# Adaptive conditioning and a mixture of experts: rows of h turned by VectorE instead of TensorE, logits turned by transposes

## The chip, the cores and the metric

The kernel runs on one core of a Trainium2 chip. The metric is the time of one execution on the device in microseconds (us), taken as the median of several runs. Engines are named as in the profile: PE is TensorE (PEld its weight loads), DVE is VectorE, ACT is ScalarE, POOL is GpSimd, SP is SyncE, which here only issues DMAs.

## The reference, cut to what matters

There are 8192 tokens (128 batches of 64) of 512 features. First a conditioning layer gives h, then an expert layer works on h, and x is added.

```python
q_emb = relu(q @ W3 + b3)
h = relu(((n * v + v_sum) * q_emb[:, None, :]) @ W2 + b2)      # v is x, v_sum over the 64 tokens of a batch
scores = softmax(h @ gate_w.T); topk_w, topk_i = top_k(scores, 6)   # 64 experts
# each expert takes its first 64 tokens in order; the others are dropped
y = sum over the kept (token, expert): topk_w * (silu(h @ w_gate[e]) * (h @ w_up[e])) @ w_down[e]
shared = silu(h @ sw_gate) * (h @ sw_up) @ sw_down             # 704 wide
out = x + y + shared
```

## The kernel before

The tokens are worked through in 16 chunks of 512. Matrix products in full precision are made of three products of parts: each operand is split in a high part (`hh`, `xmh`, `w2h`) and the rest (`hl`, `xml`, `w2l`), and `three` (L1107 to L1109) adds high x high, high x low, low x high.

The first stage goes through the chunks in pairs a, b (`body`). For each chunk PE turns x (`transpose_x`, L1117), DVE makes the modulated input (`take_xt`, with L781, L788, L796, L800), ACT and DVE split it, and PE forms h transposed, features on the partitions, in four tiles of 128 features (`cond_tile`). ACT takes each tile out of PSUM with bias and relu into `h32` (L594) and copies it to `hh` (L578); DVE makes `hl = h32 - hh` (`split_h`, by the helper line L760). The gate's logits come from `logits_raw` (L1151 to L1155), whose 128 output rows are the high and low part of the gate's weights times hh, with hl times the high part added to the first 64; ACT copies them to `lsb`, and `logits` (L1165) turns them and adds the two halves at once by a product with `fold`, two identities on top of each other. `route` on DVE finds the best six experts, z is the logits less their maximum, ACT exponentiates it, `score` normalises. `merge` keeps the first 64 tokens of each expert. PE then runs the shared expert's gate and up tiles (`gu_tile`, 11 a chunk) and down tiles (`down_tile`, four) for the odd chunks; for the even ones h is stored to `hT` and their shared expert is done in the second stage.

The second stage also needs h with tokens on the rows, as rows of a `table` in DRAM from which POOL gathers the tokens of two experts at a time. That is what `rows_tile` is for: for each of the four feature tiles of a chunk PE makes four transposes of 128x128 out of `h32` into bank 7, ACT copies them to `hrow` (`take_rows`), and after four tiles SP stores 1 MB (`store_rows`).

Each engine's program is an order written out by hand, with semaphores between them. An engine works strictly in its order. For the odd chunk b of a pair PE has: cond_tile 0, logits of a, cond_tile 1, rows_tile 0, cond_tile 2, rows_tile 1, cond_tile 3, rows_tile 2, one down_tile, a transpose of x, rows_tile 3, another transpose, logits_raw, gate and up tiles. DVE has: route of a, two split_h, score of a, split_h 2, merge 5, split_h 3, merge 6, take_down, merge 7, take_xt of the next chunk, route of b. For an even chunk c PE has cond_tile 0 and 1, rows_tile 0, two transposes of x, cond_tile 2, rows_tile 1, cond_tile 3, rows_tile 2, down_tile 0, rows_tile 3, logits_raw; DVE has score, split_h 0 and 1, take_xt, split_h 2 and 3.

In the first 70 us weights are loaded in seven pieces and split: ACT copies the high part, POOL subtracts (L528). The first piece is W2 (`w2h`, `w2l`), the last two `sdh` and `sdl`. take_cond on ACT is held until the zero rows are stored (`pads_stored`).

Of the kernel before, what the change touches and what calls it, by code (L numbers as in the profile page):

```python
# [7 lines left out]
ALU = mybir.AluOpType  # L8
# [6 lines left out]
CAP = 64  # L15
EXP_UNDERFLOW = -87.3365447
# [4 lines left out]
def adaln_moe_ffn_kernel(nc, x, cond, W3, b3, W2, b2, gate_w, w_gate, w_up, w_down,  # L21
# [42 lines left out]
    with ctx:  # L64
# [50 lines left out]
        hrow = keep("hrow", [P, J, D])  # L115
# [15 lines left out]
        fold = keep("fold", [P, E])  # L131
# [47 lines left out]
        zrows = hrow[0:CAP, :, :].rearrange("p j d -> p (j d)")  # L179
# [3 lines left out]
        class Sems:  # L183
# [16 lines left out]
            fold_ready = sem("fold_ready")  # L200
# [11 lines left out]
            rows_filled = sem("rows_filled")  # L212
# [53 lines left out]
        sgv = sw_gate.rearrange("(kc p) i -> p kc i", p=P)  # L266
        suv = sw_up.rearrange("(kc p) i -> p kc i", p=P)
# [6 lines left out]
        pieces = [([(w2v, stage_view(0, KC, D))], [(w2h[:, :, :], w2l[:, :, :], stage_view(0, KC, D))])]  # L274
# [70 lines left out]
        def _(sp):  # L345
# [14 lines left out]
            def load_hT(u):  # L360
                sp.wait_ge(s.hT_stored, 16 * (u + 1))
                if u == 0:
                    sp.wait_ge(s.rows_filled, KC * NCH)
# [50 lines left out]
            with nc.allow_non_contiguous_dma(reason="two vectors of 512 elements, once"):  # L414
                sp.dma_start(b3c[:, :], b3.rearrange("(k p) -> p k", p=P)).then_inc(s.bias_loaded, 16)
                sp.dma_start(b2c[:, :], b2.rearrange("(k p) -> p k", p=P)).then_inc(s.bias_loaded, 16)
# [61 lines left out]
            sp.wait_ge(s.rows_stored, 16 * NCH)  # L478
# [35 lines left out]
        def _(pool):  # L514
# [40 lines left out]
            pool.wait_ge(s.rows_stored, 16 * NCH)  # L555
# [20 lines left out]
        def _(act):  # L576
# [9 lines left out]
            def take_cond(n, oc):  # L586
                act.wait_ge(s.cond_filled, KC * n + oc + 1)
                wait(act, s.rows_filled, KC * (n - 1) + oc + 1)
# [62 lines left out]
            act.wait_ge(s.pads_stored, 32)  # L651
# [3 lines left out]
            take_rows(0, 0)  # L655
            take_cond(0, 2)
            take_rows(0, 1)
# [3 lines left out]
            take_rows(0, 2)  # L661
            take_lraw(0)
            take_rows(0, 3)
# [3 lines left out]
            def body(i):  # L667
# [5 lines left out]
                take_rows(b, 0)  # L673
                take_cond(b, 2)
                take_rows(b, 1)
# [3 lines left out]
                take_rows(b, 2)  # L679
                if i == 0:  # L680
                    split_piece(6)
                take_rows(b, 3)
# [23 lines left out]
                if more:  # L706
# [3 lines left out]
                    take_rows(c, 0)  # L710
                    take_cond(c, 2)
                    take_rows(c, 1)
# [3 lines left out]
                    take_rows(c, 2)  # L716
                    split_xm(d, 2)
                    take_rows(c, 3)
# [39 lines left out]
        def _(dve):  # L758
# [48 lines left out]

            def split_h(n, oc):
                dve.wait_ge(s.hh_ready, KC * n + oc + 1)
# [40 lines left out]
            def route(n):  # L850
                lg = logits_bank(n)[:, 0:J * E].rearrange("p (j e) -> p j e", j=J)
                dve.wait_ge(s.logits_filled, n + 1)
                for j in range(J):
# [5 lines left out]
                link(nc.vector.tensor_tensor(z[:, :, :], lg, top[:, :, 0:1].to_broadcast([P, J, E]), ALU.subtract))  # L859
# [166 lines left out]
            def slot_rows():  # L1026
# [11 lines left out]
            nc.vector.tensor_copy(fold[0:E, :], ident[0:E, 0:E]).then_inc(s.fold_ready, 1)  # L1038
            nc.vector.tensor_copy(fold[E:P, :], ident[E:P, E:P]).then_inc(s.fold_ready, 1)
# [10 lines left out]
                  gw2[:, :, 0:E]).then_inc(s.gw2_ready, 1)  # L1050
            split_h(0, 0)
# [53 lines left out]
        def _(pe):  # L1105
# [29 lines left out]
            def rows_tile(n, oc):  # L1135
                pe.wait_ge(s.cond_taken, KC * n + oc + 1)
                wait(pe, s.rows_taken, KC * n + oc)
                if oc == 0 and n >= 2:
                    pe.wait_ge(s.merge_step, MERGE_STEPS * (n // 2 - 1) + 1)
                for j in range(J):  # L1140
                    op = nc.tensor.transpose(bank[7][:, j * P:(j + 1) * P], h32[:, oc, j * P:(j + 1) * P], ident[:, :])  # L1141
                op.then_inc(s.rows_filled, 1)

            def logits_raw(n):
# [4 lines left out]
                for k in range(KC):  # L1149
                    if k == KC - 1:  # L1150
                        nc.tensor.matmul(o[0:E, :], gw2[:, k, 0:E], hl[:, k, :], start=False, stop=False)  # L1151
                        op = nc.tensor.matmul(o[:, :], gw2[:, k, :], hh[:, k, :], start=False, stop=True)
                    else:
                        nc.tensor.matmul(o[:, :], gw2[:, k, :], hh[:, k, :], start=(k == 0), stop=False)  # L1154
                        nc.tensor.matmul(o[0:E, :], gw2[:, k, 0:E], hl[:, k, :], start=False, stop=False)  # L1155
                op.then_inc(s.lraw_filled, 1)

            def logits(n):
# [28 lines left out]
            def ranksT(i):  # L1187
                pe.wait_ge(s.ranks_ready, 2 * i + 2)
                pe.wait_ge(s.rows_taken, KC * (2 * i + 2))
# [222 lines left out]
```

## Time and profile before

| what | value |
|---|---|
| median of 3 runs | 1317.76 us (1317.4 to 1317.92) |
| the profiled execution | 1318.17 us |
| its span in the profile | 1316.3 us |
| mean granted clock of PE | 0.993 |
| busy: PE, DVE, ACT, POOL | 1291.7, 663.3, 370.2, 169.2 us |
| HBM traffic over the span | 196 GB/s |

The profile is of one execution. Busy times are sums over the instructions of an engine; matmuls are pipelined, so a row's mean duration is longer than the pitch from one to the next, and the pitch is read from the chain of work or from starts in the timeline. PEclk is the granted clock of PE as a share of 2.4 GHz. First stage: to about 680 us; second stage: the rest.

### The profile page before, as it was taken

What the parts mean: (1) busy time and instruction counts of PE and PEld (TensorE: products, weight loads), DVE (VectorE), ACT (ScalarE), POOL (GpSimd) and SP (SyncE); (2) the same over time, 40 slices, a digit from 0 to 9 for tenths busy, and PEclk for the clock granted to TensorE, in tenths of its full rate; (3) what the DMA queues carried; (4) which work ended last, traced back from release to release, by engine and by line L of the source; (5) the groups of instructions that cost most, each with busy time, mean ns of one, the idle gap of its engine ahead of it and who ended that gap; (6) DMA issues with size and microseconds to landing.
All of it is one profiled execution on the core that took longest, in us unless ns stands there. A gap on an engine that the chain in (4) does not pass through costs nothing.

```text
span 1316.3 us, 16591 instructions
## 1 busy us (share of the span) xinstructions
PE 1291.7 (98%) x6424; PEld 962.8 (73%) x6424; DVE 663.3 (50%) x1430; ACT 370.2 (28%) x611; POOL 169.2 (13%) x129
## 2 busy tenths in 40 slices
PE   4899999999999999999999999999999999999999
PEld 3688888888888888888876666666666667666666
DVE  6685785857758577684742323223232232323322
ACT  2734443343433434334322112111121111211111
POOL 2400000000000000000001222222222222222220
PEclk7999999999999999999999999999999999999999
DMA  6434305142150522503666897997989889798952
GB/s 199 166 111 141 123 37 174 55 172 93 53 194 18 176 89 76 188 5 140 230 209 216 256 320 243 307 317 221 317 291 282 285 268 333 233 298 281 292 138 76
DMA packets 97006, 250.94 MB, mean 191 GB/s; under 512 B 17632, under 2 KB 17760, under 8 KB 94752
## 3 DMA queue, kind: packets, MB, share of 16 engines
q1 hardware_dynamic: 85440, 224.70, 47.9%
q0 software_dynamic: 11488, 25.17, 9.5%
q8 instruction: 52, 0.85, 0.3%
q14 instruction: 26, 0.21, 0.0%
HBM read 197.14 MB, written 61.10 MB: 196 GB/s over the span
## 4 chain that ended last, share of the span: by engine, by line
PE 97%; DVE 1%; ACT 1%; DMA 0%; issue 0%; SPq 0%; ACTq 0%; DVEq 0%
PE bank L1107 23%; PE bank L1109 22%; PE bank L1108 22%; PE bank L1331 12%; PE bank L1354 7%; PE bank L1141 2%; PE bank L1117 2%; PE bank L1313 1%; PE bank L1215 1%; PE bank L1214 1%; PE bank L1165 1%; PE bank L1154 1%; PE bank L1155 1%; PE bank L1340 1%; DVE xm L800 0%; DMA w3s<-in_L_cond_W_dram 0%
## 5 line engine op out<-in xcount | busy, mean ns | idle before, releaser
L1107 PE MATMUL bank<-hh,gu 128*128 128x512 f32 x704 | 281.3, 400 | 0.0
L1109 PE MATMUL bank<-hh,gu 128*128 128x512 f32 x704 | 274.6, 390 | 0.0
L1108 PE MATMUL bank<-hl,gu 128*128 128x512 f32 x704 | 274.3, 390 | 0.0
L1107 PEld LDWEIGHTS bank<-hh,gu 128*128 128x128 f32 x704 | 132.5, 188 | 38.0 <-issue 12.8
L817 DVE TENSOR_TENSOR prod<-bank,prod 128x512 f32<-128x512 f32 x96 | 66.3, 690 | 176.8 <-PE bank L1109 156.5
L1109 PEld LDWEIGHTS bank<-hh,gu 128*128 128x128 f32 x704 | 132.1, 188 | 28.6
L1108 PEld LDWEIGHTS bank<-hl,gu 128*128 128x128 f32 x704 | 132.4, 188 | 25.3
L578 ACT ACTIVATE ah<-prod 128x512 fp32r<-128x512 f32 x96 | 60.6, 632 | 262.0 <-DVE prod L817 262.0
L1107 PE MATMUL bank<-sdh,ah 128*128 128x512 f32 x320 | 128.2, 401 | 0.0
L1109 PE MATMUL bank<-sdh,al 128*128 128x512 f32 x320 | 124.9, 390 | 0.0
L1108 PE MATMUL bank<-sdl,ah 128*128 128x512 f32 x320 | 124.8, 390 | 0.0
L533 POOL DMA_INDIRECT hg<-table,idx_pair x32 | 33.1, 1033 | 704.5 <-DVE idx_hi L1029 606.4
L1107 PE MATMUL bank<-xmh,w2h 128*128 128x512 f32 x256 | 105.4, 412 | 1.8 <-DVE xml L760 1.3
L621 ACT ACTIVATE prod<-bank 128x512 f32<-128x512 f32 x96 | 57.3, 597 | 176.1 <-PE bank L1109 175.9
L1109 PE MATMUL bank<-xmh,w2l 128*128 128x512 f32 x256 | 101.3, 396 | 0.0
L1108 PE MATMUL bank<-xml,w2h 128*128 128x512 f32 x256 | 100.8, 394 | 0.0
L1354 PE MATMUL bank<-wd,eactT 128*64 128x512 f32 (+1 forms) x384 | 89.6, 601 | 0.0
L760 DVE TENSOR_TENSOR hl<-h,hh 128x512 fp32r<-128x512 f32 x96 | 66.8, 717 | 41.5 <-ACT hh L578 41.1
L594 ACT ACTIVATE h<-bank,b2c 128x512 f32<-128x512 f32 x64 | 44.0, 687 | 137.2 <-PE bank L1109 137.2
L1331 PE MATMUL bank<-wg,hgt 128*64 128x352 f32 x512 | 81.2, 459 | 0.0
L1331 PE MATMUL bank<-wu,hgt 128*64 128x352 f32 x512 | 81.2, 459 | 0.0
L1084 DVE TENSOR_SCALAR ysc<-bank,hg 64x512 f32<-64x512 f32 x64 | 48.0, 750 | 61.2 <-PE bank L1354 56.1
(123 smaller groups left out, 1705.8 us busy)
## 6 DMA issues: line engine op xcount, KB each, us to landing
wg<-in_L_ffn_w_gate_dram SPq DMA_DIRECT2D x64, 704.0 KB, 9.2
wu<-in_L_ffn_w_up_dram SPq DMA_DIRECT2D x64, 704.0 KB, 11.2
wd<-in_L_ffn_w_down_dram SPq DMA_DIRECT2D x64, 512.0 KB, 5.3
x<-in_x_dram SPq DMA_DIRECT2D x16, 1024.0 KB, 8.7
table<-hrow SPq DMA_DIRECT2D x16, 1024.0 KB, 4.4
wd<-in_L_ffn_w_down_dram SPq DMA_DIRECT2D x64, 192.0 KB, 6.1
out_dram<-outst SPq DMA_DIRECT2D x36, 256.0 KB, 3.4
hT<-h SPq DMA_DIRECT2D x8, 1024.0 KB, 3.9
```

Of the source, the lines that this page charges most:

```text
L533: nc.gpsimd.indirect_dma_start(out=hg[p % 3][:, :], out_offset=None, in_=table, in_offset=bass.IndirectOffsetOnAxis(ap=idx_pair[:, p:p + 1 ...
L578: return nc.scalar.activation(o, i, ACT.Copy)
L594: nc.scalar.activation(h32[:, oc, :], bank[5 + oc % 2][:, :], ACT.Relu, bias=b2c[:, oc:oc + 1]).then_inc(s.cond_taken, 1)
L621: nc.scalar.activation(prod[0:m, i % 2, :], bank[t % 3][0:m, :], ACT.Silu).then_inc(s.silu_ready, 1)
L760: return nc.vector.tensor_tensor(o, full, high.bitcast(F32), ALU.subtract)
L817: nc.vector.tensor_tensor(prod[0:m, i % 2, :], bank[t % 3][up0:up0 + m, :], prod[0:m, i % 2, :], ALU.mult).then_inc(s.prod_ready, 1)
L1084: op = nc.vector.tensor_scalar(ysc[p % 3][rows, :], bank[6][rows, :], hg[p % 3][rows, at:at + 1], None, ALU.mult)
L1107: nc.tensor.matmul(o, st_h, mv_h, start=first_mm, stop=False)
L1108: nc.tensor.matmul(o, st_h, mv_l, start=False, stop=False)
L1109: return nc.tensor.matmul(o, st_l, mv_h, start=False, stop=last_mm)
L1331: op = nc.tensor.matmul(o[half, 0:I], hgt[:, k, half], w[p % 2][e][:, k * I:(k + 1) * I], start=(k == 0), stop=(k == KC - 1))
L1354: op = nc.tensor.matmul(bank[6][half, :], eactT[0:m, it, half], wd[e][0:m, it, :], start=(it == 0), stop=(it == IT - 1))
```

## The change

- `rows_tile` on PE and `take_rows` on ACT are gone. DVE transposes `h32` in squares of 32x32 (`take_rows` in DVE's program, 128x512 per feature tile), before the split_h operation of the same tile, with the output written at a step of four elements. `store_rows` puts the squares in place with four DMAs in runs of 128 elements.
- So that the four feature tiles interleave to plain rows, output feature q*4+o of W2 goes to tile o, partition q: W2 is read with a step of four when it is split, b2, the gate's weights and the shared expert's weights are read in the same order.
- `logits_raw` multiplies hl with all 128 columns of the gate's weights. `logits` makes four plain transposes of 128 columns; `fold` is gone, and `route` adds the two halves with a copy out of PSUM and an add into `lg`, which is in SBUF. z is made from `lg`.
- The wait for `pads_stored` moves from ACT to DVE, before its first split_h. `ranksT` waits for the merge of the pair before.

```diff
-        hrow = keep("hrow", [P, J, D])
+        hrow = keep("hrow", [P, CH // SQ, P])
...
-        sgv = sw_gate.rearrange("(kc p) i -> p kc i", p=P)
+        sgv = sw_gate.rearrange("(p kc) i -> p kc i", p=P)
...
-        pieces = [([(w2v, stage_view(0, KC, D))], [(w2h[:, :, :], w2l[:, :, :], stage_view(0, KC, D))])]
+        pieces = [([(w2v, stage_view(0, KC, D))], [(w2h[:, :, :].rearrange("p k (o q) -> p k o q", o=KC),
+                                                    w2l[:, :, :].rearrange("p k (o q) -> p k o q", o=KC),
+                                                    stage_view(0, KC, D).rearrange("p k (q o) -> p k o q", o=KC))])]
...
-                sp.dma_start(table[n * CH:(n + 1) * CH, 0:D].rearrange("(j p) r -> p j r", p=P),
-                             hrow[:, :, :]).then_inc(s.rows_stored, 16)
+                for a in range(4):
+                    sp.dma_start(table[n * CH:(n + 1) * CH, a * P:(a + 1) * P].rearrange("(b i) c -> i b c", i=SQ),
+                                 hrow[a * SQ:(a + 1) * SQ, :, :]).then_inc(s.rows_stored, 16)
...
-            def take_rows(n, oc):
-                if oc == 0:
-                    wait(act, s.rows_stored, 16 * n)
-                act.wait_ge(s.rows_filled, KC * n + oc + 1)
-                copy(hrow[:, :, oc * P:(oc + 1) * P],
-                     bank[7][:, :].rearrange("p (j f) -> p j f", j=J)).then_inc(s.rows_taken, 1)
...
+            def take_rows(n, oc):
+
+                dve.wait_ge(s.cond_taken, KC * n + oc + 1)
+                if oc == 0:
+                    wait(dve, s.rows_stored, 64 * n)
+                nc.vector.transpose(hrow[:, :, oc:P:KC],
+                                    h32[:, oc, :].rearrange("p (b i) -> p b i", i=SQ)).then_inc(s.rows_taken, 1)
+
             def split_h(n, oc):
+                if n < NCH:
+                    take_rows(n, oc)
                 dve.wait_ge(s.hh_ready, KC * n + oc + 1)
...
             def route(n):
-                lg = logits_bank(n)[:, 0:J * E].rearrange("p (j e) -> p j e", j=J)
+
+                parts = logits_bank(n)[:, :].rearrange("p (j h e) -> p h j e", j=J, h=2)
                 dve.wait_ge(s.logits_filled, n + 1)
+                link(nc.vector.tensor_copy(lg[:, :, :], parts[:, 1, :, :]))
+                link(nc.vector.tensor_tensor(lg[:, :, :], parts[:, 0, :, :], lg[:, :, :], ALU.add))
...
-            def rows_tile(n, oc):
-                pe.wait_ge(s.cond_taken, KC * n + oc + 1)
-                wait(pe, s.rows_taken, KC * n + oc)
-                if oc == 0 and n >= 2:
-                    pe.wait_ge(s.merge_step, MERGE_STEPS * (n // 2 - 1) + 1)
-                for j in range(J):
-                    op = nc.tensor.transpose(bank[7][:, j * P:(j + 1) * P], h32[:, oc, j * P:(j + 1) * P], ident[:, :])
-                op.then_inc(s.rows_filled, 1)
...
+                    nc.tensor.matmul(o[:, :], gw2[:, k, :], hl[:, k, :], start=(k == 0), stop=False)
+                    op = nc.tensor.matmul(o[:, :], gw2[:, k, :], hh[:, k, :], start=False, stop=(k == KC - 1))
...
-                    op = nc.tensor.matmul(logits_bank(n)[:, j * E:(j + 1) * E], lsb[:, j * P:(j + 1) * P], fold[:, :],
-                                          start=True, stop=True)
+                    op = nc.tensor.transpose(logits_bank(n)[:, j * P:(j + 1) * P], lsb[:, j * P:(j + 1) * P],
+                                             ident[:, :])
```

## Rows read from the trace of the kernel before

**Rows 1.** The page: busy time of the engines, and the last chain by engine.
```profile
PE 1291.7 (98%) x6424; PEld 962.8 (73%) x6424; DVE 663.3 (50%) x1430; ACT 370.2 (28%) x611; POOL 169.2 (13%) x129
...
PE 97%; DVE 1%; ACT 1%; DMA 0%; issue 0%; SPq 0%; ACTq 0%; DVEq 0%
```

**Rows 2.** Windows: busy us (instructions) of PE, PEld, DVE, ACT, POOL; PEclk, DMA share, GB/s.
```profile
0.00:50.00 50.00, 30.76 (x137) 24.84 (x138) 32.74 (x52) 22.41 (x36) 13.76 (x14) 0.83 0.63 211
...
210.00:291.00 81.00, 81.00 (x402) 67.31 (x401) 56.24 (x134) 31.10 (x51) 0.00 (x0) 1.00 0.31 109
...
700.00:1000.00 300.00, 300.00 (x1535) 195.41 (x1534) 91.10 (x153) 50.71 (x90) 69.88 (x54) 1.00 0.85 274
...
27.00:32.00 5.00, 5.00 (x12) 3.94 (x13) 5.00 (x7) 0.67 (x2) 3.33 (x2) 0.51 0.05 3
```

**Rows 3.** The chain in order of time: start us, us, what.
```profile
14.73 5.52 DVE xm L800 x2
...
44.92 0.24 PE bank L1155
...
210.30 0.84 PE bank L1165 x8
...
213.97 0.44 PE bank L1141 x4
...
224.72 0.44 PE bank L1117 x4
```

**Rows 4.** Groups by form: count, busy us, mean ns of one, idle time before.
```profile
L1141 PE MATMUL bank<-ident,h 128*128 128x128 f32 x256 | 38.4, 272 | 1.5 <-ACT hrow L578 1.5
...
L1165 PE MATMUL bank<-fold,lsb 128*128 128x64 f32 x128 | 16.0, 268 | 0.0
```

**Rows 5.** Timeline of PE: start us, us, line, operation.
```profile
225.78 0.48 PE L1154 MATMUL bank<-hh,gw 128*128 128x512 f32 x1
...
278.27 0.48 PE L1154 MATMUL bank<-hh,gw 128*128 128x512 f32 x1
```

**Rows 6.** Timeline of DVE in a steady pair.
```profile
211.94 0.42 DVE L859 TENSOR_TENSOR z<-bank,top 128x256 f32<-128x256 f32 x1
...
213.72 0.74 DVE L868 TENSOR_SCALAR ranks<-marked,tokrank 128x64 f32<-128x64 f32 x4
...
235.28 0.68 DVE L817 TENSOR_TENSOR prod<-bank,prod 128x512 f32<-128x512 f32 x1
235.88 0.68 DVE L760 TENSOR_TENSOR xml<-xm,xmh 128x512 fp32r<-128x512 f32 x1
...
267.17 1.40 DVE L760 TENSOR_TENSOR hl<-h,hh 128x512 fp32r<-128x512 f32 x2
```

**Rows 7.** Timeline of the start, all engines.
```profile
15.19 4.51 POOL L528 TENSOR_TENSOR w2l<-stage,w2h 128x2048 fp32r<-128x2048 f32 x1 [13.37 <-ACT w2h L578]
...
44.45 0.47 PE L1154 MATMUL bank<-hh,gw 128*128 128x512 f32 x1 [1.77 <-ACT hh L578]
...
52.23 0.41 DVE L859 TENSOR_TENSOR z<-bank,top 128x256 f32<-128x256 f32 x1
52.68 2.65 DVE L860 TENSOR_SCALAR zx<-z 128x256 f32<-128x256 f32 x1
...
62.48 2.22 DVE L760 TENSOR_TENSOR hl<-h,hh 128x512 fp32r<-128x512 f32 x1 [2.30 <-ACT hh L578]
...
64.80 0.46 PE L1154 MATMUL bank<-hh,gw 128*128 128x512 f32 x1 [0.66 <-issue]
...
23.65 0.66 PE L1117 MATMUL bank<-ident,x 128*128 128x128 f32 x2 [7.75 <-DVE vsum L788]
...
60.69 3.45 POOL L528 TENSOR_TENSOR sdl<-stage,sdh 128x1536 fp32r<-128x1536 f32 x1 [5.05 <-ACT sdh L578]
```

**Rows 8.** DMA issues: KB each, us from issue to landing.
```profile
table<-hrow SPq DMA_DIRECT2D x16, 1024.0 KB, 4.4
...
table<-sc SPq DMA_DIRECT2D x16, 128.0 KB, 2.0
```

More of the change, by code:

```diff
@@ L15 @@
 CAP = 64
+SQ = 32
 EXP_UNDERFLOW = -87.3365447
@@ L128, in adaln_moe_ffn_kernel @@
         route_end = keep.at
-        fold = keep("fold", [P, E])
+        lg = keep("lg", [P, J, E])
         vsum = keep("vsum", [P, 4, KC, BPT])
@@ L178, in adaln_moe_ffn_kernel @@
         gws = cs("gws", [E, D])
-        zrows = hrow[0:CAP, :, :].rearrange("p j d -> p (j d)")
+        zrows = hrow[0:CAP, :, :].rearrange("p b c -> p (b c)")
         bank = [ctx.enter_context(nc.psum_tensor(f"bank{i}", [P, 512], F32)) for i in range(8)]
@@ L362, in load_hT @@
                 if u == 0:
-                    sp.wait_ge(s.rows_filled, KC * NCH)
+                    sp.wait_ge(s.rows_taken, KC * NCH)
                 sp.wait_ge(s.hh_ready, KC * (NCH + u))
@@ L477, in _ @@
             load_up(1)
-            sp.wait_ge(s.rows_stored, 16 * NCH)
+            sp.wait_ge(s.rows_stored, 64 * NCH)
             for n in range(2):
@@ L554, in _ @@
             pool.wait_ge(s.slots_ready, 1)
-            pool.wait_ge(s.rows_stored, 16 * NCH)
+            pool.wait_ge(s.rows_stored, 64 * NCH)
             for n in range(2):
@@ L587, in take_cond @@
                 act.wait_ge(s.cond_filled, KC * n + oc + 1)
-                wait(act, s.rows_filled, KC * (n - 1) + oc + 1)
+                wait(act, s.rows_taken, KC * (n - 1) + oc + 1)
                 wait(act, s.hl_ready, KC * (n - 1) + oc + 1)
@@ L654, in _ @@
             take_cond(0, 1)
-            take_rows(0, 0)
             take_cond(0, 2)
-            take_rows(0, 1)
             take_cond(0, 3)
@@ L660, in _ @@
                 split_xm(1, j)
-            take_rows(0, 2)
             take_lraw(0)
-            take_rows(0, 3)
             split_piece(3)
@@ L672, in body @@
                 take_cond(b, 1)
-                take_rows(b, 0)
                 take_cond(b, 2)
-                take_rows(b, 1)
                 if i == 0:
@@ L709, in body @@
                     take_cond(c, 1)
-                    take_rows(c, 0)
                     take_cond(c, 2)
-                    take_rows(c, 1)
                     take_cond(c, 3)
@@ L715, in body @@
                     split_xm(d, 1)
-                    take_rows(c, 2)
                     split_xm(d, 2)
-                    take_rows(c, 3)
                     split_xm(d, 3)
@@ L1050, in _ @@
                   gw2[:, :, 0:E]).then_inc(s.gw2_ready, 1)
+            dve.wait_ge(s.pads_stored, 32)
             split_h(0, 0)
@@ L1149, in logits_raw @@
                 for k in range(KC):
[L1150 to L1155, printed above, removed]
+                    nc.tensor.matmul(o[:, :], gw2[:, k, :], hl[:, k, :], start=(k == 0), stop=False)
+                    op = nc.tensor.matmul(o[:, :], gw2[:, k, :], hh[:, k, :], start=False, stop=(k == KC - 1))
                 op.then_inc(s.lraw_filled, 1)
@@ L1188, in ranksT @@
                 pe.wait_ge(s.ranks_ready, 2 * i + 2)
-                pe.wait_ge(s.rows_taken, KC * (2 * i + 2))
+                wait(pe, s.merge_step, MERGE_STEPS * (i - 1) + 1 if i > 0 else 0)
                 for half in range(2):
@@ L1232, in _ @@
             for k in range(KC):
-                op = nc.tensor.transpose(bank[7][:, k * E:(k + 1) * E], gws[:, k * P:(k + 1) * P], ident[0:E, 0:E])
+                op = nc.tensor.transpose(bank[7][:, k * E:(k + 1) * E], gws[:, k:D:KC], ident[0:E, 0:E])
             op.then_inc(s.gateT_filled, 1)
```

26 lines of the change are left out of this document (3 added, 23 removed).

## The prediction, made before the changed kernel had run

> **What bounds the kernel now.** I read the page first. PE works for 98% of the span, and the chain that ended last runs through PE for 97% of it [rows 1]: time is won only by taking PE work away, and lost where PE is made to wait. The windows give the stages. A steady pair of chunks (210 to 291 us) has no idle PE, DVE is busy 56 of 81 us, ACT 31. Only the start is open: PE does 30.8 of the first 50 us [rows 2]. The second stage (700 us on) is PE without a gap and contains none of the lines changed, so it should only move. The chain in order of time then gives the price of each PE step in place; the busy means (272 ns for a transpose, 1.09 for four against 0.44 in the chain) overlap and may not be multiplied [rows 3, 4].
>
> **PE: what goes.** A rows tile costs the chain 0.44 us, the longer pitch of the matmul behind it included [rows 3]. There are 64 (256 transposes, four each [rows 4]): 64 x 0.44 = 28.2 us. A logits step is 0.84 us now: its four f32 products take eight instructions (x128 for 16 chunks [rows 4]). The new one is four transposes of 128 columns, as a step of L1117, 0.44 us [rows 3]: 16 x 0.40 = 6.4 us. The products of hl with 128 columns instead of 64 stream the same 512 columns, and L1155 with its narrow weights stands in the chain with 0.24 us like the others [rows 3], so nothing. The strided transposes of gws are four, once: nothing. Together 34.6 us, if PE never waits more than before.
>
> **ACT** loses 64 copies. It is far from the bound (31 of 81 us [rows 2]), so this gives nothing by itself. In the start it ends some of PE's waits (below).
>
> **DVE: what comes.** 64 transposes of 128x512. No row shows such an operation. Below, it will not be under z's 0.42, which is for half the elements [rows 6]; above, the one place where 4-byte data takes two instructions is L1165 on PE [rows 4], and twice an xml operation is 1.4 us. The nearest row is that xml operation, as hl 128x512 f32 from SBUF to SBUF: 0.68, started 0.60 after the one before it [rows 6]. I take 0.63 per place in the queue. Each route gets a copy out of PSUM and an add of 256 elements, each with a wait on its own semaphore: as z, 0.42 + 0.03 [rows 6], so 0.9 us. The two fold copies go. Per pair that is 8 x 0.63 + 1.8 = 6.8 us more of DVE in 25 us of slack. The total fits. What matters is who waits for hl, because take_rows stands before each hl operation in the queue.
>
> *Second chunk of a pair (b), 210 us.* DVE ends ranks at 214.38 [rows 6]. The logits come 0.4 earlier and route has 0.9 more: 214.9. Two transposes and two hl (2.5) 217.4, score (1.1) 218.5, one pair 219.75, merge 5 (1.6) 221.35, the last pair 222.6. PE started logits_raw at 225.78 [rows 5]; with four rows tiles and 0.4 less it comes at 223.6. Slack 1.0 us.
>
> *First chunk (c), 260 us.* After score DVE is at 267.17 [rows 6]: two pairs 269.7, take_xt (3.75) 273.4, the last two pairs 275.9. PE came to logits_raw at 278.27 [rows 5], now 1.76 earlier, 276.5. Slack 0.6 us. So at 0.63 us a transpose costs PE nothing; from about 0.8 to 0.9 us it starts to, by four times the excess in each of the 14 later half pairs. Later steps have more: product 0 ended at 235.9 [rows 6], and gate_up tile 3 (12 matmuls of 0.23) is still ahead of tile 4, which needs it; that covers a route that is now some 1.3 us later relative to PE. The last pair has no take_xt in the queue, so its route starts when the logits are there and the slots aren't later relative to PE.
>
> **SP and DMA.** One store of 2 KB rows becomes four of 512 B runs, three issues more on SP. 512 descriptors of 256 B (the scores) land in 2.0 us, the 1 MB row store in 4.4 [rows 8]. Four groups of 512 land in 4.4 at the least and 4 x 2.0 = 8 at the most, I take 6. hrow is written again 15 us later or more: hidden. Behind it on SP stand the output stores and the x loads; the store now also starts about 3 us earlier. Hidden.
>
> **The start, where the gain is partly given back.** POOL splits weights here, and DVE operations with two SBUF inputs wait until POOL's operation ends: hl at 62.48 takes 2.22 us and ends 0.6 after POOL's 60.69 + 3.45; L800 takes 5.59 us beside POOL's w2l [rows 7]. z with one input in PSUM passed beside POOL (0.41 at 52.23), zx with one input did not (2.65 at 52.68) [rows 7]; so the transposes may wait too, but they stand beside hl operations that wait anyway, within 0.6 us of the same end.
> The Trainium skill ("SBUF — State Buffer", Who interferes with whom) calls it an exclusive lock, taken by DVE operations with two SBUF inputs or in a 2-port mode. By that, z with both inputs in SBUF is caught by it for the first time; if the move did not matter, the sum would be 0.9 us less time. The rows above agree with the rule.
> Chunk 0: logits_raw(0) already waits for ACT and DVE (idle 1.77 us [rows 7]); with the transposes it starts at about 44.6 instead of 44.45. The four tiles saved there are lost.
> Chunk 1: z now reads lg in SBUF, so it waits from 52.5 for POOL's run, which let zx through at 55.3 [rows 7], route ends near 58 instead of 57.3, then two pairs to 60.4. The multiply of score meets the sdh/sdl split starting at 60.5 and waits to 64.0; the third hl meets the second (64.3 to 68.0), and the fourth ends near 69.8. logits_raw(1) started at 64.80 [rows 7]: 5.1 us later. PE idles 61.1 to 69.9. After an idle time of 7.75 us near 20 us, 12 matmuls took 5.00 us, 0.42 each instead of 0.24, at a granted clock of 0.51, that is 1.2 GHz [rows 2, 3, 7]: 12 x 0.18 = 2.2 us, which I expect again.
> w2l: W2 is now read with a step of 16 bytes by ACT and POOL (4.51 us), and the chain at 14.73 to 20.25 is L800 waiting for POOL [rows 3, 7]. No row shows a strided POOL read. Below zero, above a doubling, 4.5 us. With no row near either end I take the middle, 2.2 us.
> The Trainium skill ("GPSIMD Engine Reference", Performance pitfalls for Q7 kernels) says that a step over 8 bytes costs 1.5 times the cycles; by it this term is 2.3 us and the sum is the same. No run so far shows it.
>
> **Sum.** Behind logits_raw(1) are 56 rows tiles (24.6) and 15 logits steps (6.0): 30.6 us gained. Given back 5.1 + 2.2 + 2.2 = 9.5; the first logits step and 8 tiles are in the wait. Net 21.1. The profiled execution took 1318.17 us (span 1316.3); minus 21.1 is 1297.1. It is 0.4 above the median of 1317.76, so the median should be 1297.
>
> **Rivals.**
> 1. *The start gives back little* (18%). The race with POOL is decided by tenths: if hl(1,2) gets in before POOL's split and w2l costs nothing, 34.6 less 2 to 4 us remain: about 1286. For it: ACT is freed of eight copies there. Against: one more transpose per hl, and z moved into SBUF.
> 2. *The transpose's strided write is slow* (14%). hrow is written with a step of 16 bytes. If its elements came at half the rate (z's 256 elements more cost 0.68 - 0.42 = 0.26 us per 256 [rows 6], so 0.52 more), it takes 1.2: 4 x 0.57 = 2.3, less a mean slack of 0.8, 1.5 us in 14 half pairs: 21 us, time 1318, no change; at one and a half, about 1305. No row in the trace has a DVE write of that step over 512 elements.
> The Trainium skill ("Advanced Engine Details and Errata", SBUF Cachelines) speaks for this one: lines of 16 bytes, and a penalty when every access meets a new line, as here. It gives no figure.
> 3. *Slower than before* (6%): the same place, but over 1.3 us each. At 1.7 us, 4 x 1.07 - 0.8 = 3.5 us in 14 half pairs is 49 us: 1346. It decides from 1.25 us on. Against it: the DVE rows of 128x512 in the steady part take 0.68 [rows 6].
> 4. *Stores too slow* (5%): if four take over 10 us, store_out and the load of x behind them come late, take_down(v,2) then route(a) hold DVE 2 to 3 us in each of 7 pairs: 1312.
> 5. The forecast as worked out has 57%, 1289 to 1304 by its own terms (w2l 0 to 4.5, lock 2 to 7, clock 0 to 3).
> Range: 1285 to 1310, which takes in rival 1 and the milder half of 2. A measurement of this kernel tells 0.2% (2.6 us) from nothing. Faster 0.88, same 0.04, slower 0.08.
>
> **What would show it.** L1141 gone from the chain, L1165 four instructions and 0.44 us a chunk; steady pairs 8 x 0.44 + 2 x 0.40 = 4.3 us shorter with PE busy throughout; the DVE transpose at 0.65 to 0.75 us; logits_raw(1) at 68 to 73 us with a long idle time before it that DVE's hl ends, granted clock near 0.5 behind it. Wrong if DVE's hl ends idle time of PE in steady pairs (transposes over 0.9), if hrow's stores hold DVE, or if the start isn't later.

## The result and the profile after

| | before | after |
|---|---|---|
| median (lowest to highest) of 4 runs each | 1317.72 us (1317.4 to 1317.92) | 1304.22 us (1301.66 to 1304.96) |
| profiled execution, its span | 1318.17, 1316.3 us | 1304.96, 1303.2 us |
| mean granted clock of PE | 0.993 | 0.986 |

The ratio is 0.9895, 95% interval 0.9882 to 0.9907: 13.5 us faster where 20.7 were forecast. Here and below, logits_raw(n) and logits(n) are the two steps of chunk n, counted from 0. The page after, with busy times, the chain by engine and the row stores:

```profile
PE 1262.3 (97%) x6104; PEld 935.7 (72%) x6104; DVE 729.9 (56%) x1524; ACT 336.9 (26%) x547; POOL 171.1 (13%) x129
...
PE 96%; issue 2%; ACT 1%; DMA 1%; DVE 0%; SPq 0%
...
table<-hrow SPq DMA_DIRECT2D x64, 256.0 KB, 4.3
```

The group of the transposes (count, busy us, mean ns of one, idle before):

```profile
L796 DVE STREAM_TRANSPOSE hrow<-h 128x512 f32<-128x512 f32 x64 | 69.6, 1087 | 0.0
```

PE is busy 29.4 us less than before [rows 1], and the span is only 13.1 us shorter: PE now waits 16 us more. Where it waits, the windows say (columns as in [rows 2]):

```profile
0.00:50.00 50.00, 26.22 (x108) 21.41 (x109) 37.62 (x54) 19.33 (x28) 13.70 (x13) 0.78 0.62 210
50.00:80.00 30.00, 20.69 (x77) 16.05 (x77) 20.82 (x41) 13.19 (x19) 13.66 (x6) 0.74 0.35 86
210.00:286.00 76.00, 75.44 (x353) 62.27 (x352) 64.38 (x146) 26.51 (x42) 0.00 (x0) 1.00 0.37 113
...
700.00:1000.00 300.00, 300.00 (x1538) 196.11 (x1538) 91.77 (x155) 51.25 (x91) 70.82 (x55) 1.00 0.87 282
```

The second stage is PE without a gap, as before. A steady pair, which had none either, now has one, and PE is idle for 33 of the first 80 us, where it was idle for 21. PE's timeline shows what stands behind the gaps; the first three rows are the start, the other two lie one pair apart:

```profile
28.39 0.77 PE L1102 MATMUL bank<-xmh,w2h 128*128 128x512 f32 x1 [1.32 <-DVE xml L743]
...
47.43 0.76 PE L1136 MATMUL bank<-hl,gw 128*128 128x512 f32 x1 [5.45 <-issue]
...
74.64 0.77 PE L1136 MATMUL bank<-hl,gw 128*128 128x512 f32 x1 [8.42 <-issue]
...
281.59 0.47 PE L1136 MATMUL bank<-hl,gw 128*128 128x512 f32 x1 [0.55 <-issue]
...
358.41 0.47 PE L1136 MATMUL bank<-hl,gw 128*128 128x512 f32 x1 [0.52 <-issue]
```

L1136 is the first product of logits_raw. It is named "issue" because several semaphores are waited for and the profile does not settle on one; DVE's timeline settles it: hl ends just ahead of each. In the start:

```profile
65.72 3.47 DVE L873 TENSOR_TENSOR sc<-ez,rsum 128x256 f32<-128x256 f32 x1
69.11 1.08 DVE L796 STREAM_TRANSPOSE hrow<-h 128x512 f32<-128x512 f32 x1
70.04 2.98 DVE L743 TENSOR_TENSOR hl<-h,hh 128x512 fp32r<-128x512 f32 x1
72.95 1.07 DVE L796 STREAM_TRANSPOSE hrow<-h 128x512 f32<-128x512 f32 x1
73.87 0.67 DVE L743 TENSOR_TENSOR hl<-h,hh 128x512 fp32r<-128x512 f32 x1
```

and POOL in the same stretch, with W2's split before it:

```profile
16.44 5.52 POOL L531 TENSOR_TENSOR w2l<-stage,w2h 128x2048 fp32r<-128x2048 f32 x1 [14.63 <-ACT w2h L581]
...
65.47 7.00 POOL L531 TENSOR_TENSOR sdl<-stage,sdh 128x1536 fp32r<-128x1536 f32 x2 [5.76 <-ACT sdh L581]
```

In the steady part, the last two pairs of operations ahead of logits_raw(c) at 127.87 us; the place that a transpose takes in the queue is read from the starts, 125.59 - 124.63 = 0.96 and 127.10 - 126.20 = 0.90 us:

```profile
124.63 1.11 DVE L796 STREAM_TRANSPOSE hrow<-h 128x512 f32<-128x512 f32 x1
125.59 0.67 DVE L743 TENSOR_TENSOR hl<-h,hh 128x512 fp32r<-128x512 f32 x1
126.20 1.05 DVE L796 STREAM_TRANSPOSE hrow<-h 128x512 f32<-128x512 f32 x1
127.10 0.67 DVE L743 TENSOR_TENSOR hl<-h,hh 128x512 fp32r<-128x512 f32 x1
```

**The two parts of the miss.** The four transposes of logits(1) start at 81.56 us, where the step stood at 69.45 before: 12.1 us later (9.5 forecast). From there to the end of the span (1303.2 and 1316.3 us) it is 1221.6 us against 1246.9: 25.2 us gained (30.6 forecast).

### The profile page after: what moved, and what is told of

It reads as the page before. It is cut to its first block, busy times and chain, and to the rows that moved or that the text cites. A ratio compares the mean times of both kernels' runs of the same rounds, so it can differ in the third digit from the quotient of the medians.

```text
span 1303.2 us, 15965 instructions
## 1 busy us (share of the span) xinstructions
PE 1262.3 (97%) x6104; PEld 935.7 (72%) x6104; DVE 729.9 (56%) x1524; ACT 336.9 (26%) x547; POOL 171.1 (13%) x129
## 4 chain that ended last, share of the span: by engine, by line
PE 96%; issue 2%; ACT 1%; DMA 1%; DVE 0%; SPq 0%
PE bank L1102 23%; PE bank L1104 22%; PE bank L1103 22%; PE bank L1300 12%; PE bank L1323 7%; PE bank L1112 2%; PE bank L1136 2%; PE bank L1137 1%; PE bank L1282 1%; PE bank L1197 1%; PE bank L1196 1%; PE bank L1309 1%; DMA stage<-in_L_cond_W_dram 1%; PE bank L1147 1%; ACT w2h L581 0%
## 5 line engine op out<-in xcount | busy, mean ns | idle before, releaser
L1060 DVE TENSOR_TENSOR eact<-bank,esilu 128x352 f32<-128x352 f32 x32 | 16.8, 525 | 102.4 <-issue 96.4
## 6 DMA issues: line engine op xcount, KB each, us to landing
wu<-in_L_ffn_w_up_dram SPq DMA_DIRECT2D x64, 704.0 KB, 10.3
```

## The experiments

Medians are of 4 runs each; the kernel before ran beside them at 1317.66 us (first four), 1318.0 (e5 to e8) and 1318.11 (e9 to e12). "Pair" is the distance from one logits_raw(c) to the next in PE's timeline, the first of them between 261 and 283 us.

| run | edit to the changed kernel, if not said otherwise | median us | ratio, 95% interval | pair us | logits(1) at us |
|---|---|---|---|---|---|
| before | | 1317.72 | | 80.50 | 69.45 |
| after | | 1304.22 | 0.9895, 0.9882 to 0.9907 | 76.82 | 81.56 |
| e1 | dense write of the transposes | 1293.74 | 0.9819, 0.9803 to 0.9836 | 75.83 | 78.07 |
| e2 | dense split of W2 | 1301.11 | 0.9871, 0.9855 to 0.9888 | 76.82 | 78.91 |
| e3 | POOL's sdl split all but left out | 1299.40 | 0.9856, 0.984 to 0.9873 | 76.89 | 76.17 |
| e4 | transposes behind the fourth hl | 1287.06 | 0.9768, 0.9752 to 0.9784 | 75.83 | 71.29 |
| e5 | kernel before, logits part alone | 1312.48 | 0.9957, 0.994 to 0.9973 | 79.56 | 70.80 |
| e6 | rows part alone | 1307.99 | 0.9928, 0.9911 to 0.9944 | 77.54 | 79.97 |
| e7 | features in runs of 32 | 1290.03 | 0.9789, 0.9773 to 0.9805 | 75.83 | 75.17 |
| e8 | e7 and e4 | 1283.25 | 0.9738, 0.9722 to 0.9754 | 75.83 | 67.70 |
| e9 | sdl split in short instructions | 1299.19 | 0.9856, 0.984 to 0.9873 | 76.87 | 75.80 |
| e10 | e8 and e9 | 1280.16 | 0.9722, 0.9706 to 0.9739 | 75.84 | 64.13 |
| e11 | e8 with e3's cut | 1279.71 | 0.9715, 0.9699 to 0.9731 | 75.84 | 64.33 |
| e12 | W2 split by its four parts | 1301.33 | 0.9875, 0.9859 to 0.9892 | 76.83 | 77.27 |

**e1: the transpose writes densely.** The theory was that the 16-byte step of the write makes the transpose long, and that this length is PE's new wait. The table's rows come out permuted.

```
-                nc.vector.transpose(hrow[:, :, oc:P:KC],
-                                    h32[:, oc, :].rearrange("p (b i) -> p b i", i=SQ))
+                at = hrow[:, :, :].rearrange("p b c -> p (b c)")[:, oc * CH:(oc + 1) * CH]
+                nc.vector.transpose(at.rearrange("p (b i) -> p b i", i=SQ),
+                                    h32[:, oc, :].rearrange("p (b i) -> p b i", i=SQ))
```

> The changed kernel, but VectorE writes each transposed tile of 128x512 as one contiguous run of hrow instead of at a step of four elements; the rows in the table come out in another order, so the experts work on permuted rows. Theory A (the step of 16 bytes in the write makes the transpose take 1.09 us instead of about 0.7): transposes 0.65 to 0.75 us, the idle time of TensorE before logits_raw in steady pairs (0.5 us a pair, 0.8 in the last) gone, logits_raw of chunk 1 some 1 to 2 us earlier, total 1296 to 1299. Rival B (the transpose of 4-byte data costs 1.09 us whatever it writes): 1.05 to 1.1 us each, total as the changed kernel, 1302 to 1305.

Group of the transposes and a steady window of e1:

```profile
L797 DVE STREAM_TRANSPOSE hrow<-h 128x512 f32<-128x512 f32 x64 | 45.0, 703 | 0.5 <-ACT h L597 0.5
```

```profile
210.00:286.00 76.00, 76.00 (x359) 63.17 (x358) 62.41 (x147) 26.51 (x42) 0.00 (x0) 1.00 0.40 120
```

1293.74 us, 10.5 less, more than was expected. The same operation takes 703 ns with a dense write and 1087 with the step, so the step costs 0.38 us an instruction. Its place in the queue is 0.63 us (a transpose at 120.47, the hl behind it at 121.10), as the forecast had it. The steady gap is gone. The span is 11.5 us shorter (1303.2 to 1291.7): 3.5 before logits(1), 8.0 behind it.

**e2: W2 split densely.** The features come out permuted (the edit takes the two rearrangements off W2's entry in pieces).

```
-        pieces = [([(w2v, stage_view(0, KC, D))], [(w2h[:, :, :].rearrange("p k (o q) -> p k o q", o=KC),
-                                                    w2l[:, :, :].rearrange("p k (o q) -> p k o q", o=KC),
-                                                    stage_view(0, KC, D).rearrange("p k (q o) -> p k o q", o=KC))])]
+        pieces = [([(w2v, stage_view(0, KC, D))], [(w2h[:, :, :], w2l[:, :, :], stage_view(0, KC, D))])]
```

> The changed kernel, but W2 is split with contiguous reads as before the change, so the features of h come out in another order than the weights behind it expect. Theory A (the strided read slows ScalarE's copy from 1.91 to 3.91 us and GpSimd's subtraction from 4.51 to 5.52, and the chain runs through both): the copy 1.9 and the subtraction 4.5 again, first matmul of chunk 0 at 26.9 instead of 28.4 us, total 1.5 us lower, near 1302. Rival B (the first matmul is late for the load of W2 or for VectorE's own work): times of the two operations fall, the start does not move by more than 0.3 us.

1301.11 us, 3.1 less. With the step ACT's w2h took 3.91 us and POOL's w2l 5.52; without it 1.91 and 4.84 (1.91 and 4.51 in the kernel before). The first product starts at 26.90 instead of 28.39.

**e3: POOL leaves the port free.** "The port" is short here for the hold-up that the prediction reads from [rows 7]: a DVE operation with two SBUF inputs lasts until the POOL instruction under way has ended. The low part of the shared expert's down weights, sdl, is left out: POOL subtracts 16 columns of each of its two pieces and sdl is zero, so DVE meets no long POOL operation from 60 us on.

```
+            nc.gpsimd.memset(sdl[:, :, :].bitcast(F32), 0.0)
...
+                    if n >= 5:
+                        h_part, l_part, src = h_part[:, 0:1, 0:16], l_part[:, 0:1, 0:16], src[:, 0:1, 0:16]
```

> The changed kernel, but GpSimd subtracts only 16 columns for each of the two pieces of the shared down weights (sdl is set to zero at the start; their low part is left out). Theory A (VectorE operations with two SBUF inputs wait for the end of GpSimd's operation): score's multiply 0.42 instead of 3.47 us, the third hl of chunk 1 0.68 instead of 2.98, logits_raw of chunk 1 at about 69 instead of 74.6 us, total 5 to 7 us lower, 1297 to 1299. Rival B (ScalarE's order and the transposes hold this place, the lock only shows): logits_raw of chunk 1 at 73 or later, total within 2 us of the changed kernel.

1299.40 us, 4.8 less, 0.4 short of the expected range. The multiply of the scores takes 0.42 us for 3.47, the third hl 0.67 for 2.98, and logits_raw(1) starts at 68.74 instead of 74.64. Not all of this is the port (see the start, below). The gap in each steady pair stays: it is another cause.

**e4: the same transposes, later in the queue.** Still with the step, everything computed; only their place differs.

```
             def split_h(n, oc):
-                if n < NCH:
-                    take_rows(n, oc)
                 dve.wait_ge(s.hh_ready, KC * n + oc + 1)
                 lower(hl[:, oc, :], h32[:, oc, :], hh[:, oc, :]).then_inc(s.hl_ready, 1)
+                if 0 < n < NCH and oc == KC - 1:
+                    for o in range(KC):
+                        take_rows(n, o)
```

(and take_rows(0, 0 to 3) behind the xml operations of chunk 1)

> The changed kernel with the order on VectorE changed: the four transposes of a chunk stand behind its fourth hl operation (for chunk 0 behind the four xml operations of chunk 1), so no hl waits for them. Complete and equal output. Theory A (what is lost in steady pairs is hl waiting behind transposes): no idle time of TensorE before logits_raw in steady pairs, both logits_raw of the start earlier (chunk 0 by about 3 us), total 1294 to 1298. Rival B (the transposes only move the wait to product, xml or route behind them): idle time turns up before gate_up tiles or before cond_tile, total 1301 to 1306.

Transposes and a steady window of e4, and its timeline of PE at two logits_raw(c) one pair apart:

```profile
L796 DVE STREAM_TRANSPOSE hrow<-h 128x512 f32<-128x512 f32 x64 | 61.9, 1087 | 0.0
```

```profile
210.00:286.00 76.00, 76.00 (x358) 63.20 (x357) 64.50 (x148) 26.60 (x43) 0.00 (x0) 1.00 0.39 116
```

```profile
268.58 0.39 PE L1139 MATMUL bank<-hl,gw 128*128 128x512 f32 x1
...
344.41 0.39 PE L1139 MATMUL bank<-hl,gw 128*128 128x512 f32 x1
```

1287.06 us, 17.2 less, 7 us better than the best that was expected. In the spans it is 18.3 us: 8.0 behind logits(1), as in e1, and 10.3 before it. DVE is as busy as in the changed kernel (64.50 us for 64.38) and PE has no gap in the steady pairs: there the length hurt only because four transposes stood ahead of hl operations that PE waits for. In the start logits_raw(1) comes at 65.10 us (71.27 in e1). Chunk 0's transposes run from 47.50 to 51.43, while DVE has nothing else to do until the logits arrive, and chunk 1's stand behind the hl. That brings the multiply of the scores ahead of POOL's split (0.42 us at 60.13, POOL from 60.96), so only the fourth hl is held (2.85 us); in e1 both the multiply (3.36) and the third hl (3.27) are. So the gain in the start is in part a race won, and not the order alone.

**e5 and e6: each part alone.** e5 is the kernel before with the new products, the four transposes and route's copy and add. e6 is the changed kernel with the old half products and folding matmuls. The edits are the hunks of the diff shown above: logits_raw, logits and route put into the kernel before, or taken back out of the changed one.

> The kernel before with the logits part alone: full products, four transposes, the two DVE operations that add the halves; the rows tiles on PE stay. Forecast's term: 16 chunks save 0.40 us of PE each = 6.4 us, less up to 0.9 us for the longer route in the start: 1311.5 to 1312.5 us. Rival: the gain is not there, because the full products cost more than a product on half the rows of the array or the route becomes late: 1316 to 1318 us.

> The changed kernel with the old logits (folding matmuls, half products): rows part alone. If the two parts add up (13.5 us together, of which about 6 the logits), this gives 1309 to 1311 us, with the idle time of about 0.5 us before every second logits_raw still there. Rival: the parts hide each other (the half products give the third hl no less time, but the old product order puts the last hl later): then part of the idle time goes and it is under 1308 us.

e5 is as expected. e6 is 1.0 us below its range, at the edge of its rival's (under 1308), but the idle time before logits_raw(c), which that rival wanted smaller, is as in the changed kernel (0.53 for 0.55). 1312.48 us is 5.5 less than its neighbour, 1307.99 is 10.0 less; together they would give 15.5, and the change gave 13.5. PE's gap before logits_raw(c) is there in e6, but a pair without its loss would be 80.50 - 3.73 (below) = 76.77 us, so e6 loses 0.77 us a pair where the changed kernel loses 1.0. With the logits part, PE comes to logits_raw sooner and DVE, with route's two operations more, later. Over 7 and a half pairs this is 1.7 of the 2.0 us. That the two parts meet in this way is read off the pairs; no run isolates it.

**e7 and e8: an order of features without the step.** Partition and column are exchanged in runs of 32, so the four transposes of a chunk write runs of 32 elements, and W2 is split in runs of 32. The loads fetch the weights to match; everything is computed.

```
-                nc.vector.transpose(hrow[:, :, oc:P:KC],
+                nc.vector.transpose(hrow[:, :, oc * SQ:(oc + 1) * SQ],
...
-        sgv = sw_gate.rearrange("(p kc) i -> p kc i", p=P)
+        sgv = sw_gate.rearrange("(a kc q) i -> a q kc i", a=4, q=SQ)
...
+        (w2h[:, k, :].rearrange("p (o a q) -> p o a q", o=KC, a=4),
+         w2l[:, k, :].rearrange("p (o a q) -> p o a q", o=KC, a=4),
+         stage_view(0, KC, D)[:, k, :].rearrange("p (a o q) -> p o a q", o=KC, a=4))   for each k of 4
```

(sw_up, b2 and the router's weights in the same way; PE waits for all four parts of W2)

> The changed kernel with another order of the features: each transpose writes runs of 32 elements that lie together, and W2 is split in runs of 32 too; the gate, up, router and b2 loads fetch the features in that order, everything is computed. If the stride of 16 bytes is the cost (10.5 us in the rows and 3.1 us in W2, by the two experiments on each), both come back: 1289.5 to 1292.5 us, transposes at about 0.70 us, POOL's w2l at about 4.8 us, no idle time in steady pairs. Rival: a run of 32 elements still costs (row by row start-up), or the loads in four pieces make the start late: over 1295 us, with transposes over 0.85 us or the first matmul over 28 us.

> The same order of features, and the transposes behind the fourth hl of their chunk. If the start is what is left beside PE's own work, W2's 3.1 us come off the 1287.1 us of the rows-last kernel, and the shorter transposes give up to 1.5 us more in the start: 1282.5 to 1284.5 us, PE busy throughout each steady pair. Rival: PE was already the bound from the first product on and the start's waits only move (POOL's down-projection split still holds the hl): 1285 to 1287 us.

Transposes of e7:

```profile
L801 DVE STREAM_TRANSPOSE hrow<-h 128x512 f32<-128x512 f32 x64 | 45.0, 703 | 1.7 <-ACT h L602 1.7
```

1290.03 and 1283.25 us, both as forecast. A run of 32 elements costs the transpose nothing: 703 ns, as dense. POOL's w2l was expected at about 4.8 us; its four instructions take 6.58. e7's start mixes two things, since W2 is also split in four instructions; e12 takes that apart.

**e9: shorter POOL instructions.** Each of the two subtractions of 128 x 1536 becomes three of 128 x 512.

```
+                    if n >= 5:
+                        for w in range(3):
+                            op = nc.gpsimd.tensor_tensor(l_part[:, w, :], src[:, w, :], h_part[:, w, :].bitcast(F32),
+                                                         ALU.subtract)
```

> The changed kernel, with POOL's two subtractions for sdl (128 x 1536, about 3.5 us each) done in three instructions of 128 x 512 each; nothing else differs and everything is computed. If DVE is held until the POOL instruction under way has ended, a held DVE instruction gets in after about 1.2 us in place of 3 to 3.5 us: the multiply of the scores and the third hl each lose 1.5 to 2.3 us of their 3 to 3.5, logits_raw(1) comes 3 to 4.5 us earlier, 1299.5 to 1302 us. Rival: POOL holds the port over a whole row of its instructions, or DVE does not get in between two of them: the durations stay at 3 us or more and the time at 1303.5 to 1305.

POOL's and DVE's timelines of e9:

```profile
63.66 8.87 POOL L533 TENSOR_TENSOR sdl<-stage,sdh 128x512 fp32r<-128x512 f32 x6 [5.00 <-ACT sdh L586]
```

```profile
64.71 0.85 DVE L878 TENSOR_TENSOR sc<-ez,rsum 128x256 f32<-128x256 f32 x1
65.49 1.11 DVE L801 STREAM_TRANSPOSE hrow<-h 128x512 f32<-128x512 f32 x1
66.44 0.81 DVE L748 TENSOR_TENSOR hl<-h,hh 128x512 fp32r<-128x512 f32 x1
```

1299.19 us, the same as with the split left out (1299.40). DVE gets in between two POOL instructions: the multiply takes 0.85 us, hl 0.81. A POOL instruction now lasts 1.3 to 1.7 us, and the multiply and hl each met one (63.66 to 65.28, 65.25 to about 66.7) in its last 0.3 to 0.6 us. That they met it so late is luck, so a hold of up to a whole short instruction has to be reckoned with. The six together take 1.9 us longer than the two did, which nobody waits for.

**e10 and e11: all of it together.** e10 is e8 with e9's edit, e11 is e8 with e3's (sdl zero), as the bound for it.

> The fastest kernel so far (1283.3 us: features in runs of 32, transposes behind the fourth hl) with sdl's subtractions in pieces of 128 x 512. The third... fourth hl there lasted 2.86 us for 0.68; if it gets in after one short piece, logits_raw(1) comes 1.5 to 2.2 us earlier and the time is 1281 to 1282 us. Rival: DVE does not get in: 1283 to 1284 us.

> The same fastest kernel with sdl left at zero (POOL subtracts only 16 columns of each of the two pieces), the bound of what freeing the port can give: fourth hl at 0.68 us, logits_raw(1) 2.2 us earlier and warm: 1280.5 to 1281.5 us. Rival: the start waits for something else then (hh, cond_taken) and it stays over 1282.5.

Page, and window of 50 to 80 us, of e10:

```profile
PE 1254.0 (98%) x6104; PEld 932.2 (73%) x6104; DVE 704.6 (55%) x1524; ACT 335.1 (26%) x550; POOL 172.0 (13%) x136
```

```profile
50.00:80.00 30.00, 28.16 (x135) 23.01 (x134) 28.37 (x74) 13.81 (x20) 10.55 (x8) 1.00 0.59 172
```

1280.16 us (1279.58 to 1283.57) and 1279.71 (1279.34 to 1281.94): both somewhat better than expected, and the same within what can be told. e10 computes everything and is the fastest version, 24 us under the changed kernel and 38 under the one before. logits_raw(1) starts at 59.50 us, and the granted clock is 1.00 throughout the window, where the changed kernel had 0.74.

**e12: W2 split in four instructions, step kept.**

```
+        [(w2h[:, k, :].rearrange("p (o q) -> p o q", o=KC),
+          w2l[:, k, :].rearrange("p (o q) -> p o q", o=KC),
+          stage_view(0, KC, D)[:, k, :].rearrange("p (q o) -> p o q", o=KC))   for each k of 4
```

> The changed kernel with W2 split in four instructions on ACT and four on POOL, one for each of its four parts, still with the 16-byte step; PE waits for all four. POOL starts behind the first of ACT's parts, 3 us earlier, so w2l ends some 2.5 to 3 us earlier though it is no cheaper; if w2l sets the first product, it starts up to 1.5 us earlier (26.9 for 28.4 us) and 1301 to 1303 us. Rival: the first product waits for xml and thus for the port that w2l holds and the whole chain of the start, and nothing is gained: 1303.5 to 1305 us.

```profile
13.99 7.61 POOL L532 TENSOR_TENSOR w2l<-stage,w2h 128x512 fp32r<-128x512 f32 x4 [12.18 <-ACT w2h L582]
```

1301.33 us, 2.9 less: POOL starts at 13.99 us instead of 16.44, behind ACT's first part, and the first product starts at 25.64 instead of 28.39, though the four take 7.61 us for 5.52. That is about as much as e2 gave back by taking the step away. e7's first product starts at 26.00 us, no earlier than with the step: there ACT's first part starts at 14.54 us for 12.78 here, behind the load of W2, which in e7 stands behind four loads of the router's weights for one. How much of e7's start is the shorter run's and how much the split in four, these runs leave open.

## Why the prediction was off by 7 us

By the profiled executions the miss is 7.9 us (1304.96 against 1297.1): 2.6 before logits(1) and 5.4 behind it. The stated range held only because it took in the milder half of rival 2. The forecast's own terms were said to reach 1304; added up (4.5 + 7 + 3 = 14.5 given back of 30.6) they reach 1302 at the most, and 1304.22 lies outside. PE's work was also worth 2.6 us more than priced (below), which hides as much of the loss.

**PE's work: right in kind, a little too small.** With no loss, a pair is 75.83 us (e1, e4) against 80.50 before: 4.67 us, forecast 4.32. e5 splits it: the logits part takes 80.50 - 79.56 = 0.94 us from a pair, 0.47 a step for 0.40; the rest is 3.73 us for eight rows tiles, 0.47 each for the 0.44 read from the chain. From logits(1) to the end, e4 (span 1284.9 us) needs 1284.9 - 71.29 = 1213.6 us, 33.2 less than before, where I had worked out 30.6.

**The transpose's length: the step that failed.** "I take 0.63 per place in the queue", from hl's row, because both are 128x512 f32 from SBUF to SBUF. Its place was 0.90 to 0.96 us. e1 shows that the operation itself was priced well (703 ns, against hl's 0.68) and that the 16-byte step of its write was the missing 0.38. I had this as rival 2, with 14%: its milder half, one and a half times 0.63, is 0.94. The prediction's own sign of being wrong came true with it: DVE's hl ends idle time of PE in steady pairs, with transposes over 0.9.

**What the length costs: the reckoning held.** I had slacks of 1.0 us (b) and 0.6 us (c) and four transposes ahead of each. With 0.94 in place of 0.63 that gives 4 x 0.31 = 1.24: 0.24 us lost in b and 0.64 in c, 0.9 a pair. Measured: 76.82 - 75.83 = 1.0 us a pair. At c the pitch from the last product of down_tile (280.65) to logits_raw (281.59) is 0.94 us for a pitch of 0.23, so 0.7 us is lost; the other 0.3 lies before logits_raw(b), where the row shows no idle time: from c to b it is 25.87 us (281.59 to 307.46) and 25.54 in e4 (268.58 to 294.12), and the two transposes of x just ahead of b take 1.02 us there (306.44 to 307.46) for 0.79 in e4. With the last pair it makes 1221.6 - 1213.6 = 8.0 us. So the place was wrong and the rest of that step right: 33.2 - 8.0 = 25.2.

**The start: 12.1 us for a forecast of 9.5.** It falls into three stretches. Up to DVE's first transpose of chunk 1 the forecast was 58 us and 2.2 for w2l, 60.2; it started at 62.02, 1.8 later. From there to logits_raw(1) it was 11.9 (58 to 69.9); it took 12.6 (to 74.64). The clock behind it was 2.2; it was 2.3. The 1.8 and the 0.7 are the miss of 2.6, up to rounding.
- A second stretch at the low clock, which the prediction did not have. logits_raw(0) was forecast at 44.6 us and started at 47.43, after 5.45 us of idle PE. From it to logits(0) the changed kernel takes 9.10 us (47.43 to 56.53) and e4, with the same products and 2.21 us of idle time ahead of them, 5.81 (45.27 to 51.08). The granted clock of that window is 0.50 in the one (1.2 GHz) and 1.00 in the other. The windows of both, and the one behind logits_raw(1), first the changed kernel's:

```profile
48.00:53.00 5.00, 4.11 (x10) 2.80 (x9) 1.72 (x3) 1.78 (x3) 0.00 (x0) 0.50 0.88 198
73.00:78.00 5.00, 3.36 (x8) 2.71 (x9) 5.00 (x11) 0.00 (x0) 0.00 (x0) 0.50 0.58 129
```

```profile
48.00:53.00 5.00, 4.75 (x23) 3.97 (x24) 4.64 (x9) 4.04 (x7) 3.76 (x3) 1.00 0.12 28
```

logits(0) so starts 6.3 us later than before (56.53 for 50.26). Not all of that reaches DVE's queue: before, zx waited 2.65 us for POOL [rows 7], and now the route came when that POOL run was nearly over.
- The port. The multiply, the third hl and their order were as forecast; they took 3.47 and 2.98 us. From the first transpose of chunk 1 to logits_raw(1) it is 12.6 us, and 7.3 in e3 (61.44 to 68.74) and 8.1 in e9 (60.96 to 69.04): the port is worth 5.3 and 4.5 us there. These two runs start logits_raw(1) 5.9 and 5.6 us earlier; the other 0.6 and 1.1 us are there at that first transpose already, before POOL reaches sdl, and go with a shorter stretch at the low clock (logits(0) at 54.30 and 53.82). The kernel before paid a part of the port too (zx, and its fourth hl, 2.22 us), so 5.3 is not to be set against the forecast of 5.1, which is a difference to that kernel.
- W2: e2 starts the first product 1.5 us and logits_raw(1) 2.7 us earlier (71.98). I priced only POOL's w2l, at 2.2 us; against e2 it grew by 0.7 (4.84 to 5.52), while ACT's w2h, ahead of it on the same path, grew by 2.0 (1.91 to 3.91) and was not in the sum. The total came out near for the wrong reason.
The Trainium skill ("GPSIMD Engine Reference", Performance pitfalls for Q7 kernels) would have put POOL's operation at one and a half times its cycles; 5.52 us is 1.14 times e2's 4.84 and 1.22 times the 4.51 of before, which doesn't agree (one of its two operands is read with the step, the other and the result are dense).
- The transposes' length: e1 starts logits_raw(1) 3.4 us earlier (71.27). This was no term of the start at all, since I let the transposes hide beside hl operations that wait anyway. They don't all, and eight stand ahead of logits_raw(1), each 0.38 us longer for the step. 2.3 of the 3.4 us are there at the first transpose of chunk 1 (59.73), with a shorter stretch at the low clock among them (7.29 us from logits_raw(0) to logits(0)); 1.1 come behind it.
- The clock behind logits_raw(1): from there to logits(1) it took 6.9 us (74.64 to 81.56) and 4.6 in e10 (59.50 to 64.13), where the granted clock stayed at 1.00. PE had stood idle 8.42 us. That is 2.3 us, forecast 2.2.

The effects of the single edits overlap: 5.9, 2.7 and 3.4 us add up to 12.0, and logits_raw(1) came only 9.8 us later than before.

**The lock.** "The transposes may wait too": they don't. The one at 69.11 us takes its 1.08 while POOL splits, the one at 65.49 in e9 1.11; each has a single SBUF input. z, now with both inputs in SBUF, was meant to be caught; it took 0.73 us at 59.26 (0.42 in steady pairs), because by then POOL's run was at its end (59.71). What was held were the multiply and hl, with two SBUF inputs each.
The Trainium skill ("SBUF — State Buffer", Who interferes with whom) lets these two kinds fall apart in just this way, and the trace agrees: two-input operations 3.47 and 2.98 us beside POOL, 0.42 and 0.67 without it (e3). It also has the lock held for one whole instruction at a time, which e9 bears out.

**Costed at nothing, and rightly so.** The full products of hl (e5's pair is 0.94 us shorter, where 0.80 was worked out with these products at no cost). The stores: each of the four lands in 4.3 us, the one before in 4.4 [rows 8], and though they hold SP for 3.1 us and DVE waits longer for x at take_down (29.0 us in all, 9.4 before, 49.9 in e4), e4 has the same stores and no idle PE in steady pairs. That DVE waits so was one of the prediction's signs of being wrong ("if hrow's stores hold DVE"); it is there and costs PE nothing. The rival of slow stores is out.

**The rivals.** Rival 1 (1286) needed the race with POOL won and W2 free; the race was lost, as forecast. e4 won it for the multiply, and came to 1287. Rival 2's mechanism is what moved the result; at its "one and a half" it gave about 1305, and 1304.22 was measured. That this fits so well is partly luck: by the rival's own rule (4 x 0.31 less a mean slack of 0.8, in 14 half pairs) the figure is 1303, and the 2.6 us that the start lost and the 2.6 us that PE gained beyond the forecast cancel. Rival 3 is out: the transposes stayed under 1.25 us.
The Trainium skill ("Advanced Engine Details and Errata", SBUF Cachelines) spoke for rival 2, and the trace agrees with it in direction: one access to each line of 16 bytes costs 1087 ns against 703; runs of 32 elements (e7) cost nothing.

## What to carry to other kernels

Moving work from the bound engine to an idle one is worth its full price only if the new work does not stand ahead of something the bound engine waits for; look first at whether it can be queued behind that (17 us here, with not one operation made faster, 8 of them in the steady pairs). Price each operation in its new layout on every engine that touches it, and choose an order of elements whose inner runs are long, if loads can fetch it. Where DVE meets POOL, short POOL instructions returned nearly all that leaving the POOL work out would (e9 against e3, e10 against e11).

## What the runs showed of the hardware that I had not expected

- DVE's f32 transpose of 128x512 is as quick as a subtraction of that size (703 ns against 0.68 us, 0.60 from one to the next in e10's row of four), and a write with a step of 16 bytes makes it 1.55 times as long.
- The same step in an ACT copy of 128x2048, read from SBUF, doubles it (1.91 to 3.91 us), but lengthens POOL's subtraction by 0.7 to 1.0 us only (4.84 in e2 and 4.51 before, to 5.52).
- DVE's hold-up beside POOL is counted by instruction: beside short ones of 1.3 to 1.7 us a DVE operation became 0.43 us longer at the most (0.85 for 0.42, 0.81 for 0.67), where one of 3.5 us held it 2.3 to 3.1 us.
- Four stores of 512 runs of 512 bytes hold SP for 3.1 us, 0.78 each (at 127.28 us), and still land in the time of a single store of 1 MB.
